# Expert weights split two chunks ahead, their low halves on GpSimd, and the gate's weights held in the array

## The reference, cut to what matters

```
x = x + attention parts
n = layernorm(x)                                   # 512 tokens x 512
gate_logits = n @ W_gate                           # 512 x 8
top_w, top_idx = top_k(gate_logits, 2); top_w = softmax(top_w)
for e in range(8):
    h = gelu(n @ W_in[e] + b_in[e])                # 512 -> 2048, exact gelu
    y = h @ W_out[e] + b_out[e]                    # 2048 -> 512
    out += combine[:, e] * y                       # zero for tokens that did not choose e
x = x + out
```

## Time and profile before

| | us |
|---|---|
| median of 3 runs (lowest, highest) | 1291.79 (1289.74, 1292.31) |
| the profiled execution, its own time | 1289.2 |
| its span in the trace | 1287.4 |
| PE busy | 1235.0 |
| DVE busy | 970.4 |
| ACT busy | 825.9 |
| POOL busy | 141.6 |

### The profile page before, as it was taken

One profiled execution on the slowest core, in us unless ns is written; L12 is line 12 of the kernel. 1 busy time (PEld: TensorE's weight loads), 2 busy tenths in 40 slices (PEclk: granted clock), 3 DMA queues, 4 the chain that ended last, 5 costly groups with the idle time before them and its releaser, 6 DMA issues. The chain is left out here.

```text
span 1287.4 us, 22815 instructions
## 1 busy us (share of the span) xinstructions
PE 1235.0 (96%) x9352; PEld 722.2 (56%) x9352; DVE 970.4 (75%) x851; ACT 825.9 (64%) x1085; POOL 141.6 (11%) x124
## 2 busy tenths in 40 slices
PE   7999999999999999999999999997878999999997
PEld 5555555555555555555555555552566766666664
DVE  6567777777777877777777777787755788788785
ACT  4677777767767677777776767675224666665653
POOL 0110100101001010010100101000012011111112
PEclk9999999999999999999999999999996999999999
DMA  5501101011010110100101000002523777777761
GB/s 196 198 2 34 34 1 34 1 34 33 2 34 2 34 33 2 34 3 31 33 2 34 14 21 1 1 21 95 184 81 119 245 258 249 249 256 241 240 213 57
DMA packets 56379, 107.91 MB, mean 84 GB/s; under 512 B 5874, under 2 KB 6002, under 8 KB 56272
## 3 DMA queue, kind: packets, MB, share of 16 engines
q1 hardware_dynamic: 53568, 101.55, 23.1%
q0 software_dynamic: 2720, 5.09, 1.7%
HBM read 95.57 MB, written 12.14 MB: 84 GB/s over the span
## 5 line engine op out<-in xcount | busy, mean ns | idle before, releaser
L527 DVE TENSOR_TENSOR p_sum<-p_sum,as_p 128x2048 f32<-128x2048 f32 x252 | 577.2, 2291 | 182.7 <-ACT as_p L494 181.8
L494 ACT ACTIVATE as_p<-as_s 128x1024 f32<-128x1024 f32 x512 | 496.2, 1022 | 122.0 <-PE as_s L423 122.0
L438 PE MATMUL as_o<-as_p,as_v 128*32 128x512 f32 x2048 | 247.1, 599 | 1.6 <-DVE o_acc L535 1.4
L375 POOL TENSOR_TENSOR as_c_lo<-as_c,as_c_hi 128x512 fp32r<-128x512 f32 x60 | 78.9, 1316 | 683.6 <-ACT as_c_hi L486 683.6
L423 PEld LDWEIGHTS as_s<-as_q_hi,as_k_hi 32*128 32x128 f32 x1024 | 49.4, 182 | 159.3 <-issue 146.7
L423 PE MATMUL as_s<-as_q_hi,as_k_hi 32*128 32x512 f32 x1024 | 129.5, 494 | 4.4 <-ACT as_p L494 3.6
L438 PEld LDWEIGHTS as_o<-as_p,as_v 128*32 128x32 f32 x2048 | 53.2, 109 | 124.8 <-issue 120.8
L423 PE MATMUL as_s<-as_q_lo,as_k_hi 32*128 32x512 f32 x1024 | 104.0, 391 | 0.0
L423 PE MATMUL as_s<-as_q_hi,as_k_lo 32*128 32x512 f32 x1024 | 103.8, 390 | 0.0
L1212 ACT ACTIVATE se_h<-se_ht,se_b_cur 128x128 f32<-128x128 f32 x128 | 36.6, 369 | 87.7 <-PE se_ht L1109 87.5
L1228 DVE TENSOR_TENSOR se_wi_lo<-ei_wi,se_wi_hi 128x2048 fp32r<-128x2048 f32 x32 | 73.3, 2290 | 18.7 <-ACT se_wi_hi L1187 18.7
(11 more groups left out here) (258 smaller groups left out, 1611.9 us busy)
## 6 DMA issues: line engine op xcount, KB each, us to landing
ei_wi<-w_in SPq DMA_DIRECT2D x32, 1024.0 KB, 5.3
ei_wo<-w_out SPq DMA_DIRECT2D x32, 1024.0 KB, 7.1
as_c<-ctx_t SPq DMA_DIRECT2D x16, 1024.0 KB, 5.2
slots_scratch<-as_zeros SPq DMA_DIRECT2D x10, 256.0 KB, 5.1
acc_scratch<-as_zeros SPq DMA_DIRECT2D x10, 256.0 KB, 4.8
pq_w<-xw_in SPq DMA_DIRECT2D x1, 2048.0 KB, 10.5
se_tokens<-slots_scratch SPq DMA_DIRECT2D x7, 256.0 KB, 7.5
x_sb<-x SPq DMA_DIRECT2D x4, 256.0 KB, 3.2
```

Of the source, the lines that this page charges most:

```text
L375: nc.gpsimd.tensor_tensor(c_lo[b][:, d, :], c[:, d, :], c_hi[b][:, d, :].bitcast(F32), ALU.subtract).then_inc(c_lo_ready, 1)
L438: last = nc.tensor.matmul(o[j * D:(j + 1) * D, :], v[b][:, t, feats], p[step % PR][:, j * NQ:(j + 1) * NQ], start=(t == 0), stop=(t == KT ...
L494: nc.scalar.activation(p[step % PR][:, pair * 2 * NQ:(pair + 1) * 2 * NQ], s[r][:, :], ACT.Exp, scale=SCALE).then_inc(p_ready[step % PR], 1)
L527: nc.vector.tensor_tensor(sums, sums, p[step % PR][:, :], ALU.add).then_inc(p_summed[step % PR], 1)
```

## The change

Four things are edited.

**Where the low halves of the first layer are made.** DVE makes only those of chunks 0 and 1. POOL makes the other thirty, 128x2048 each, in its one program between the loads of `meta` and the scatters: in the turn of expert e those of the four chunks of expert e+1, the third ahead of the scatter of `y`, the fourth between the two scatters (and chunks 2 and 3 of expert 0 ahead of all).

**When the high halves are made.** ACT makes `wi_hi` of chunk n+2, not n+1, in chunk n, as soon as `hidden` of n is done, behind `wo_hi` and ahead of the gelus. DVE's order within a chunk becomes: `pre`, (`tail_y`), `wo_lo`, (`xg_lo`), `tail_pre`, (`y`), `h_hi`, `h_lo`.

**The gate.** The 8 gate columns are the weights in the array and the 128 tokens of a tile move; the result is 8 rows of 512 tokens. ACT copies them to `gate_t`, four PE transposes turn them back, and only then comes `x_hi` on ACT.

**Idle streams.** Twelve constant matmuls follow the gate's transposes, and six stand ahead of `gather`.

In `route`, PE's gate and what follows it:

```diff
                 for d in range(ET):
-                    last = nc.tensor.matmul(gate[:, t * NX:(t + 1) * NX], xt[:, d, t * P:(t + 1) * P], wg[:, d, :],
+                    last = nc.tensor.matmul(gate_rows[0:NX, t * P:(t + 1) * P], wg[:, d, :], xt[:, d, t * P:(t + 1) * P],
                                             start=(d == 0), stop=(d == ET - 1))
             last.then_inc(gated, 1)
+            pe.wait_ge(gate_kept, 1)
+            for t in range(QT):
+                last = nc.tensor.transpose(gate[:, t * NX:(t + 1) * NX], gate_t[:, t * P:(t + 1) * P], ident[0:NX, 0:NX])
+            last.then_inc(turned_back, 1)
+            if idle is not None:
+                stream_idle(nc, pe, idle, gate_rows[:, :], 12)
```

In `route`, ACT and DVE:

```diff
+            act.wait_ge(gated, 1)
+            nc.scalar.activation(gate_t[:, :], gate_rows[0:NX, :], ACT.Copy).then_inc(gate_kept, 1)
             nc.scalar.activation(r.x_hi[:, :, :], xn[:, :, :], ACT.Copy).then_inc(hi_ready, 1)
...
-            dve.wait_ge(gated, 1)
+            dve.wait_ge(turned_back, 1)
```

In `send_to_experts`, POOL's program, and PE's `gather`:

```diff
+            def split_in(n):
+                e, mc = n // NMC, n % NMC
+                pool.wait_ge(wi_hi_ready, n + 1)
+                nc.gpsimd.tensor_tensor(wi_lo[mc % 2][:, :, :], wi[mc][:, :, :], wi_hi[mc % 2][:, :, :].bitcast(F32),
+                                        ALU.subtract).then_inc(wi_lo_ready, 1)
+
...
+                if e == 0:
+                    split_in(2)
+                    split_in(3)
                 if e < NX - 1:
-                    for rows, which, ready in ((y, meta, y_ready), (tail_y, tail_meta, tail_y_ready)):
+                    split_in(NMC * (e + 1))
+                    split_in(NMC * (e + 1) + 1)
+                    for k, (rows, which, ready) in enumerate(((y, meta, y_ready), (tail_y, tail_meta, tail_y_ready))):
+                        split_in(NMC * (e + 1) + 2 + k)
                         pool.wait_ge(ready, e + 1)
...
+                stream_idle(nc, pe, idle, ht[:, 0, :], 6)
```

In `send_to_experts`, a chunk of ACT, then a chunk of DVE:

```diff
-                    if not (last and mc == NMC - 1):
-                        wait_reuse(act, h_done, 2 * n)
-                        split_in(e + (mc + 1) // NMC, (mc + 1) % NMC)
+                    wait_reuse(act, y_done, n - 1)
+                    split_out(e, mc)
...
+                    if not (last and mc >= NMC - 2):
+                        act.wait_ge(h_done, 2 * n + 1)
+                        split_in(e + (mc + 2) // NMC, (mc + 2) % NMC)
...
-                    if not (last and mc == NMC - 1):
-                        split_in(e + (mc + 1) // NMC, (mc + 1) % NMC)
                     keep_hidden(n)
...
+                    if mc == 1 and not first:
+                        keep_tail(e - 1, e)
+                    wait_reuse(dve, y_done, n - 1)
+                    split_out(n, mc)
...
+                    keep_hidden_tail(n)
```

More of the change, by code:

```diff
@@ L131, in stream_idle @@
     for _ in range(count):
-        nc.tensor.matmul(bank[:, :], idle.tile[:, 0:P], idle.tile[:, :], start=True, stop=True)
+        nc.tensor.matmul(bank, idle.tile[:, 0:P], idle.tile[:, :], start=True, stop=True)
 def norm_transpose(nc, pe, xn, ident, banks, ready, turned):
@@ L246, in _ @@
             if idle is not None:
-                stream_idle(nc, pe, idle, proj[NG - 1], 24)
+                stream_idle(nc, pe, idle, proj[NG - 1][:, :], 24)
             pe.wait_ge(ident_made, 1)
@@ L680, in _ @@
             if idle is not None:
-                stream_idle(nc, pe, idle, proj[ET - 1], 20)
+                stream_idle(nc, pe, idle, proj[ET - 1][:, :], 20)
             norm_transpose(nc, pe, xn, ident, turn, normed, turned)
@@ L771, in route @@
     ranks = ctx.enter_context(nc.psum_tensor(u + "ro_ranks", [P, (QT + 1) * NX + 1], F32))
-    spare = ctx.enter_context(nc.psum_tensor(u + "ro_spare", [P, NQ], F32))
+    gate_rows = ctx.enter_context(nc.psum_tensor(u + "ro_gate_rows", [P, NQ], F32))
+    gate_t = sb("ro_gate_t", [NX, NQ])
     turned_weights = ctx.enter_context(nc.psum_tensor(u + "ro_turned_weights", [NX, NQ], F32))
@@ L775, in route @@
         "ro_var_ready", "ro_root_ready", "ro_small", "ro_chain", "ro_normed", "ro_turned", "ro_xt_ready"))
+    gate_kept, turned_back = map(sem, ("ro_gate_kept", "ro_turned_back"))
     made, gated, link, gap_ready, ratio_ready, masked, unmasked = map(sem, (
@@ L815, in _ @@
             if idle is not None:
-                stream_idle(nc, pe, idle, spare, 20)
+                stream_idle(nc, pe, idle, gate_rows[:, :], 20)
             norm_transpose(nc, pe, xn, ident, turn, normed, turned)
@@ L934, in send_to_experts @@
 def send_to_experts(nc, ctx, opened, w_in, b_in, w_out, ident, x_sb, out_dram, r, inputs, slots_dram, acc_dram, sent, meta_loaded, landed,
-                    last_loaded):
+                    last_loaded, idle):
     sb = lambda n, s, d=F32: ctx.enter_context(nc.sbuf_tensor(f"se_{n}", s, d))
@@ L1201, in expert @@
                         nc.scalar.activation(xg_hi[:, :, :], turn[:, :, 0:CAP], ACT.Copy).then_inc(xg_hi_ready, 1)
-                    wait_reuse(act, y_done, n - 1)
-                    split_out(e, mc)
+                    if not (last and mc >= NMC - 2):
+                        act.wait_ge(h_done, 2 * n + 1)
+                        split_in(e + (mc + 2) // NMC, (mc + 2) % NMC)
                     if mc == NMC - 1 and not last:
@@ L1221, in _ @@
             nc.scalar.activation(xg_hi[:, :, :], turn[:, :, 0:CAP], ACT.Copy).then_inc(xg_hi_ready, 1)
+            split_in(0, 1)
             rolled(act, NX, expert)
@@ L1284, in expert @@
                     n, b = NMC * e + mc, mc % 2
-                    if not (last and mc == NMC - 1):
-                        split_in(e + (mc + 1) // NMC, (mc + 1) % NMC)
                     keep_hidden(n)
-                    if mc == 0:
-                        keep_hidden_tail(n)
+                    if mc == 1 and not first:
+                        keep_tail(e - 1, e)
+                    wait_reuse(dve, y_done, n - 1)
+                    split_out(n, mc)
+                    if mc == NMC - 1 and not last:
+                        dve.wait_ge(xg_hi_ready, e + 2)
+                        nc.vector.tensor_tensor(xg_lo[:, :, :], turn[:, :, 0:CAP], xg_hi[:, :, :].bitcast(F32),
+                                                ALU.subtract).then_inc(xg_lo_ready, 1)
+                    keep_hidden_tail(n)
                     if mc == 0 and first:
@@ L1295, in expert @@
                         keep_rows(e - 1, e)
[L1296 to L1305, removed]
                     for t in range(0, MT, 2):
@@ L2202, in perceiver_layer @@
                 send_to_experts(nc, s, experts, w_in, b_in, w_out, ident, x_sb, out, r, inputs, slots_dram, acc_dram, sent, meta_loaded,
-                                landed, last_loaded)
+                                landed, last_loaded, idle)
         any_path(nc, whole, experts, stored, landed, again, dram, ident, x_sb)
```

## The result

The changed kernel takes 1342.61 us (median of 4 runs, 1339.96 to 1343.81), the kernel before 1290.9: the ratio is 1.0395, with 95% between 1.0378 and 1.0412. It is slower, by 52 us. The span of the profiled execution grew from 1287.4 to 1340.0, by 52.6. One microsecond of that lies ahead of `route`, which begins at 949.2 in place of 948.2 although nothing before it is edited. Over the profiled executions of all versions that start lies between 946.8 and 952.9, for a reason that no run shows. So where versions differ by a few us, the time from `route`'s start to the end is given beside the median; here it grew by 51.6.

What follows compares the result with a forecast made beforehand. PE was taken as the bound, 34.2 us of work in a 36.3 us expert. To 1289.2 us were added start 7.4, the turn before the full ones 1.5, five full turns 38, last expert 4: 1340 us, range 1300 to 1360.

Steps and rivals of the forecast that it cites:

- front: Ahead of the experts: gate, x_lo and idle streams together move their start by -2.0 to +3.1 us, taken as 0.
- start, to expert 1: Expert 0: POOL's first half, behind scatters, landing and meta, makes chunk 2 late by 6.4 us; with blocking, 7.4.
- last expert: Expert 7: has the cycle's three halves in a row but no landing behind it, +4 us.
- Off DVE: Expert loop: 30 subtractions, some 68 us, leave DVE; PE can gain at most 2.1 us an expert.
- no exclusion: Rival, expert loop: POOL and DVE don't exclude each other at this size; 34.2 us an expert, 1281 us total; chance 0.13.
- giving way inside an instruction: Rival, expert loop: POOL yields mid-instruction, DVE pieces wait 1.15 us at most; 39 an expert, 1313 total; chance 0.27.
- The cycle: Expert loop: late POOL halves and DVE pieces close into a 43.9 us turn against 36.3, 7.6 more an expert.
- Step 1: Chunk 3's h_hi and h_lo get in singly between three successive POOL halves: 14.5 us.
- Step 6: POOL's queue: fourth half 4.6, then tail's scatter 1.4, landing 5.1, issue of meta 1.15, its wait 3.2 us.
- The gate, x_lo and the streams: Before the experts: gate path +1.2 us, x_lo +0.5, streams between -3.7 and +1.4; together taken as 0.
- the rule weighed: POOL against DVE: the second instruction fully blocks until the first finishes; with it 1340 us, without it 1314.
- the likeliest case: Expert loop: the cycle as summed, 1325 to 1358 us for the kernel, chance 0.50.

Runs made afterwards that it cites:

- experiment 1: The changed kernel with DVE making all low halves of the first layer, each behind h_lo of the chunk two before: 1276.86 us, ratio 0.9886.
- experiment 10: The changed kernel's experts with DVE making all low halves, the gate as in the kernel before and no idle streams: 1273.07 us, ratio 0.9869.
- experiment 4: The changed kernel with h_hi and h_lo made 128x512 at a time, two instructions a chunk, still from memory: 1330.46 us, ratio 1.0316.
- Experiment 6: The changed kernel with DVE making the low halves of chunks 2 and 3 of expert 0: 1333.6 us, ratio 1.0326.
- experiment 7: The kernel before with only the change's new gate, twelve and six idle streams: 1289.35 us, ratio 0.9993.
- experiment 5: The changed kernel with meta loaded once before the loop and the landing waited for only ahead of the next expert's y scatter: 1303.62 us, ratio 1.0108.
- experiment 12: The changed kernel, POOL making 28 halves: meta loaded once, gelus in their bank, expert 0's chunks 2 and 3 on DVE, x_hi before gate_t: 1274.5 us, ratio 0.9882.
- 11: The changed kernel with DVE making all low halves and ACT making x_hi ahead of gate_t: 1270.02 us, ratio 0.9843.
- experiment 3: The changed kernel with gelus of the main rows kept in their bank, h_hi and h_lo made from there, 128x512 each: 1304.39 us, ratio 1.0101.

## Why the prediction came out

The forecast, 1340 us and slower by late halves that exclude DVE's pieces, holds. Its terms do not all have the size I gave them; three were too small, the largest too large. That these errors cancel and the total comes out to within 3 us is luck. What was right is the mechanism: halves that come late and hold DVE off.

| term | predicted | in the trace |
|---|---|---|
| front | 0 | 979.75 - 977.83 = 1.9 |
| start, to expert 1 | 7.4 | 13.4 - 1.9 = 11.5 |
| expert 1 to 2 | 1.5 | 37.9 - 36.3 = 1.6 |
| five full turns | 5 x 7.6 = 38 | 43.9 - 15.0 = 28.9 |
| last expert | 4 | 59.9 - 51.1 = 8.8 |
| sum | 51 | 52.6 |

- *Off DVE.* Right: without the halves DVE would give PE its 34.2 us an expert; experiment 1 shows 34.6. The 15 us that I set as the most for the loop is about what experiment 10 gains from `route`'s start to the end, 15.9.
- *The price of a half.* 4.49 the shortest, 4.75 the median, 6.45 the longest (taken 4.58).
- *Exclusion for the whole instruction.* Right: 4.62 and 4.75 for an `h_lo` of 0.43. The rivals of no exclusion and of giving way inside an instruction fall with these rows, and experiment 4 shows that it is no matter of their number. The rule of the Trainium skill, page "SBUF — State Buffer", section "Who interferes with whom", agrees with these durations.
- *The cycle.* That late halves and DVE's pieces close into a longer turn is right; the path through it was not the one I laid out. Step 1 had three halves back to back and PE waiting some 8 us for the last `h_lo`. But the third half waits 0.71 for its high half, the second `h_hi` and `h_lo` slip into that gap, all four pieces end 6.3 us after the first two gelus (1152.97 to 1159.25), and PE waits 1.50 and 2.38. That sign of being right did not come, except in the last turn (6.94). What I did not have is `b_cur`: the third half reaches PE through it and `tail_pre`, and 4.1 of the 5.8 us that an expert lost lie there, between chunk 0 and chunk 1 (12.95 for 8.83). Most of the rest is the wait of 1.50 for the half. In experiment 4, where `b_cur` gets through, `wo_lo` is held by the third half in its place (6.13). No run takes `b_cur` away alone. Step 6 had 3.2 for `meta`'s wait: it is 4.5 to 5.5. The `y` scatter takes 1.66, not 3.0. In all 42.1 for 43.9, in part by luck.
- *The last expert.* Mis-sized: both `h_lo` are held, and expert 7 takes 18.0 us from chunk 0 to chunk 1. The third half starts 0.57 behind the second, 0.03 ahead of the second `h_lo`; in the five full turns that `h_lo` came first, by 0.09 to 0.13. A tenth of a us decides which of the two waits.
- *The start.* The mechanism is right and the size too small. Chunk 2 starts at 1012.92, not 1007.4, because the queue passed the second load of `meta` at 1003.59, not at 999.63 (the front, a scatter of 2.35 for 0.96, a later landing), and because its wait was 4.78 for 3.2. `hidden` of chunk 2 then ran at a granted clock of 0.50, and chunk 3 came 9.6 behind it, not 8.2. Experiment 6 measures 9.0.
- *The gate, x_lo and the streams.* The gate's passes take 3.66 (3.64 in the earlier trace rows): no change, as taken. The marks cost 3.0 us and `ro_gap`, no longer held, gives 0.8 back: 2.2, where I took 0.5 and had 2.7 as the bound. The six streams ran at half clock, 2.72 for the 2.6 I reckoned, and the gather gained 1.1 and 1.7. That these cancel, taken as 0, is borne out by experiment 7; of the 1.9 in the table 1.0 lies ahead of `route`.
- *Two slips* that change nothing: the rule weighed speaks of the second rival's 1314 where the first one's 1313 is meant, and the stated bounds give some 1351 for the likeliest case's upper end, not 1358.

## What to carry to other kernels

Work that is moved to an idle engine is priced by when it can start there, more than by its length: the same halves cost 52 us behind a landing and a load, 13 with these out of their way (experiment 5), and with every repair they still gain nothing over DVE making them (experiment 12 against 11). Before a POOL instruction on memory is put beside DVE's chain, lay out which short DVE steps are waited for, and either let these read from a bank or keep the halves clear of them. An order that lets an engine finish what is waited for first, and puts the long subtraction behind it, was worth 16 to 18 us without any second engine (experiment 10).

## What the runs showed of the hardware

A DVE instruction need not have two operands in memory to be held: `b_cur` (128x16, a tensor_scalar) took 4.22 where it takes 0.16, and the `h_hi` casts up to 1.66 for 0.29 (4.67 in experiment 6). Of the instructions that read a bank none was seen held. `tail_pre` lay wholly within a half 16 times in the changed kernel and took 0.29 at most, and `xg_lo`, a subtraction with one operand in a bank, 6 times and took its 0.82. In experiment 3 `h_hi` lay there 21 times and `h_lo` 11 times, at 0.69. The Trainium skill, page "SBUF — State Buffer", section "Who interferes with whom", says that casts and tensor_scalar can contend, in modes that use both of VectorE's ports, and that tensor_tensor does so with two inputs in memory; these rows agree with both.

In two places where both engines had work they took turns, an instruction each: four quarters let four DVE pieces through at 1.24 to 1.36 each, and eight marks of 128x8, 0.15 apart when free, took 4.89 us beside four pieces of `x_lo`.
